# Left and right products of a two-layer pair block: token pairs side by side in the projection's columns, tokens in natural order

## The chip, the cores and the metric

One core of a Trainium2 chip runs one program. The metric is the device time of one execution in microseconds (us). The kernel before was run three times: 113.83, 113.94 and 114.15 us, median 113.94 us.

## What is computed

The input x has shape (1, 128, 128, 32), read as 128 x 128 tokens of 32 channels. Two layers follow each other; everything is float32.

```
# layer 0
x   = layernorm(x0) * ln1_w + ln1_b
left  = sigmoid(x @ left1) * (x @ left2)
right = sigmoid(x @ right1) * (x @ right2)
p   = einsum('nsre,nkre->nske', left, right)     # contraction over r, for each feature e
p   = layernorm(p) * ln2_w + ln2_b
q   = (p @ out_w) * sigmoid(x @ gate)
x1  = x0 + q
# layer 1
left = x1 @ W_left + b_left + x1 @ W_eq + b_eq
right_sum = sum over r of (x1 @ W_right + b_right)
out = left * right_sum * sigmoid(x1 @ W_gate + b_gate)
y   = layernorm(out @ W_out + b_out + x1) * ln_scale + ln_bias
```

## The kernel before

**Tiling.** The partition is r (128 rows), so `x_tok[r, s, c]` holds token s of row r in 32 neighbouring floats. The 128 tokens s are worked through in 8 chunks of 16 (`SPC`). Four tokens times 32 channels fill the 128 columns of one TensorE transpose, so a chunk is four blocks of four tokens.

**Who does what is written out by hand.** Each engine has its own program (`@block.sync`, `gpsimd`, `scalar`, `vector`, `tensor`), in which the instructions stand in the order written, and counting semaphores tie them together. No scheduler or planner moves anything. SP (the sync engine) issues the loads of x in order of the table `SUMS1` (two halves of chunk 0, then whole chunks), ACT one of them and the weights.

**First stretch, layer 0 up to the products.** For each chunk: VectorE (DVE) takes statistics of two tokens at a time (L581, `statistics1`); ACT takes square roots (L410), DVE reciprocals (L588); GpSimd (POOL) subtracts the mean (L281, `centre`) and scales (L288, `normalise1`), for the first half chunk DVE does (L608, L613); TensorE (PE) transposes the four blocks into a PSUM bank (L802, `transpose_xn`); ACT writes `xnT` to SBUF with weight and bias (L421, `affine1`); PE projects it for left and right (L817, `project_lr`), half a chunk (8 tokens) at a time; ACT takes the sigmoid of half of the columns (L431, `sigmoid_lr`); DVE multiplies the other half with it and writes `lr` (L596, `multiply_lr`). So there are 16 projections, 16 sigmoids and 16 products of 128 x 512 elements, numbered j = 2c + h for chunk c and half h. Three pairs of PSUM banks are used in turn: projection j waits until product j - 3 is done (`lr_ready`).

**One projection.** A projection has four matmuls. Each takes 64 rows of `xnT` (two tokens of 32 channels) as weights and streams `lr_blk`, 64 x 256, in which each of the two tokens has its own 128 columns: left1, right1, left2, right2, 32 columns each. The output is token by token: 128 neighbouring columns for one token.

```
596  lr[:, :, s].rearrange("p f s -> p s f")      # L596, the product's output
816  dst = bank[:, 2 + 2 * (j % 3) + t].rearrange("p (g n f) -> p n g f", g=2, n=2)[:, n]   # L817's output
```

**The layout of `lr`.** `lr[r, feature, s]` has 64 features (32 left, 32 right) and, for each, 128 neighbouring tokens, because the contraction over r (L871) takes `lr[:, e, :]` as a 128 x 128 operand: 32 matmuls of layer 0, one per feature. They wait for all 16 products (`lr_ready`, 16). The product of half a chunk thus writes 8 tokens x 64 features, feature innermost, and from one element to the next the address moves by 128 floats.

**Order of the tokens before.** So that the four matmuls of a half chunk leave their 8 tokens in order in the two banks, each chunk of 16 tokens is stored in SBUF with its 8 even tokens first and its 8 odd ones behind them (`place`, `even_first`, `stat`, `in_order`). The loads fetch even and odd tokens apart (L250, L398); everything that touches `x_tok`, `xc`, `t_tok`, the statistics of layer 0 and the columns of `xnT` lives with that order. `in_order` puts the tokens right again where the last projections write to PSUM (L967, L978, L987), in runs of 32 columns.

**After the products.** ACT copies the eight banks of p to `p_sb` (L465), DVE takes its statistics (L660), POOL (L352; chunk 0: DVE, L673) scales it and turns it to token order as `t_tok`, PE transposes it (L912) and projects it (L923), DVE adds gate and residual (L688, L697), and layer 1 follows in a loop over the 8 chunks (L992), where PE is busy most of the time. At the end the last two chunks' outputs are made by PE once more, scaled (L987), and DVE and POOL finish (L739, L785, L376).

Of the kernel before, what the change touches and what calls it, by code (L numbers as in the profile page):

```python
# [30 lines left out]
P = 128  # L31
CH = 32
GRP = P // CH
# [38 lines left out]
def place(tokens, lo, hi):  # L72

    rest = tokens.rearrange("p (m q) c -> p m q c", q=SPC // 2)
    if hi - lo < SPC:
        c, h = lo // SPC, lo % SPC // (SPC // 2)
        return rest[:, 2 * c:2 * c + 2, GRP * h:GRP * h + GRP]
    return rest[:, 2 * lo // SPC:2 * hi // SPC]


def arrived(b):

    lo, hi = SUMS1[b]
    return 32 * max(1, (hi - lo) // SPC)
# [7 lines left out]
def pair_layers(nc, x, weights, rows, out):  # L92
# [7 lines left out]
    with ExitStack() as ctx:  # L100
# [12 lines left out]
        pair_mask = sb("pair_mask", [P, 2, CH])  # L113
        lr_blk = sb("lr_blk", [P, 2, 4, CH])
# [96 lines left out]
        def halves(cols, lo, hi):  # L211

            v = cols.rearrange("p (n h k) -> p n (h k)", n=2, h=2)
            if hi - lo == SPC:
                return v
            h = lo % SPC // (SPC // 2)
            return v[:, :, h * P:(h + 1) * P]

        def even_first(features):

            return features.rearrange("p e (q n) -> p n q e", n=2)

        def stat(row, lo, hi):

            return place(row.rearrange("p (s a) -> p s a", a=1), lo, hi)

        def mean_of(lo, hi):

            v = place(stats1[:, :, 1:2], lo, hi)
            return v.to_broadcast([P, v.shape[1], v.shape[2], CH])  # L230

        def each_feature(row, lo, hi):
            v = stat(row, lo, hi)
            return v.to_broadcast([P, v.shape[1], v.shape[2], CH])
# [27 lines left out]
        def _(pool):  # L262
# [11 lines left out]
            for g in range(GRP):  # L274
                pool.wait_ge(consts, 1 + GRP + g)
                nc.gpsimd.memset(pair_mask[g * CH:(g + 1) * CH, g % 2, :], 1.0).then_inc(consts, 1)

            def centre(b):
                lo, hi = SUMS1[b]
                pool.wait_ge(stats1_ready, b + 1)  # L280
                nc.gpsimd.tensor_tensor(place(xc[:], lo, hi), place(x_tok[:], lo, hi), mean_of(lo, hi),  # L281
                                        ALU.subtract).then_inc(centred1_pool, 1)

            def normalise1(n):
# [3 lines left out]
                nc.gpsimd.tensor_tensor(place(xc[:], lo, hi), place(xc[:], lo, hi),  # L288
                                        each_feature(rstd[:, 0], lo, hi), ALU.mult).then_inc(xn_pool, 1)

            def block_diagonal(dst, src):
# [104 lines left out]
        def _(act):  # L396
            lo, hi = SUMS1[0]
            act.dma_start(place(x_tok[:], lo, hi)[:, 1], x_tok_dram[:, lo + 1:hi:2, :]).then_inc(x_in[0], 16)  # L398
# [5 lines left out]
            def root(layer, lo, hi, done):  # L404
                values, of = std[:, layer, lo:hi], st[:, layer, lo:hi]
                if layer == 0:
                    values, of = stat(std[:, 0], lo, hi), place(stats1[:, :, 2:3], lo, hi)
# [632 lines left out]
```

## Time and profile before

| | |
|---|---|
| three runs | 113.83, 113.94, 114.15 us |
| span of the profiled execution | 112.1 us |
| its own device time | not given beside the span; 1.84 us lie between the span and the median of the runs |
| PE busy | 92.5 us (83%) |
| DVE busy | 77.3 us (69%) |
| ACT busy | 66.6 us (59%) |
| POOL busy | 62.6 us (56%) |
| the 16 products (L596) on DVE | 15.9 us |
| load of x | until about 18.4 us |

The span runs from the first to the last instruction on the core. A busy share is taken over the whole span, so what a shorter instruction is worth is to be read from its own stretch: from what ends last there.

### The profile page before, as it was taken

How to read it: one execution, taken by the hardware profiler on the slowest of the kernel's cores; microseconds unless marked ns; L12 is line 12 of the kernel's file. 1: busy time of each engine (PE TensorE's matmuls, PEld its weight loads, DVE VectorE, ACT ScalarE, POOL GpSimd, SP SyncE). 2: the span in 40 equal slices, each digit the busy share in tenths (PEclk: the TensorE clock that was granted, in tenths of full speed). 3: DMA queues.
4: the chain of work that ended last, by engine and by line, in shares of the span. 5: the costliest groups of instructions: out<-in, count | busy, mean ns of one | idle time of the engine just before them, and what ended most of it. 6: DMA issues, size and time to landing. Idle time of an engine off the chain costs nothing. (4 is left out here: it accounts for less than half of the span.)

```text
span 112.1 us, 1886 instructions
## 1 busy us (share of the span) xinstructions
PE 92.5 (83%) x600; PEld 72.3 (64%) x600; DVE 77.3 (69%) x284; ACT 66.6 (59%) x110; POOL 62.6 (56%) x78
## 2 busy tenths in 40 slices
PE   1997599789999899999979999999999996495000
PEld 1994368567776799545445789878877994394000
DVE  1528697986769800599975869699979963996500
ACT  0614888687785166795499463993797399330000
POOL 5037974599950040025488585587865492699400
PEclk9999999999999999999999999999999999999955
DMA  3669997000000000000000000000023006029996
GB/s 60 126 111 171 146 146 75 0 0 0 0 0 9 0 0 0 0 0 3 0 0 0 3 6 0 0 0 6 0 35 59 0 0 94 0 34 144 147 144 100
DMA packets 33486, 4.54 MB, mean 40 GB/s; under 512 B 33348, under 2 KB 33476, under 8 KB 33476
## 3 DMA queue, kind: packets, MB, share of 16 engines
q1 hardware_dynamic: 31632, 4.00, 27.6%
q10 hardware_dynamic: 1844, 0.41, 1.8%
q8 instruction: 5, 0.08, 0.3%
q14 instruction: 5, 0.04, 0.1%
HBM read 2.31 MB, written 2.10 MB: 39 GB/s over the span
## 5 line engine op out<-in xcount | busy, mean ns | idle before, releaser
L596 DVE TENSOR_TENSOR lr<-bank,sig_lr 128x512 f32<-128x512 f32 x16 | 15.9, 1044 | 3.7 <-ACT sig_lr L431 3.7
L817 PE MATMUL bank<-lr_blk,xnT 64*128 64x256 f32 x128 | 16.5, 392 | 1.0 <-ACT xnT L421 0.7
L352 POOL TENSOR_TENSOR t_tok<-p_sb,rstd 128x512 f32<-128x512 f32 x7 | 10.2, 1462 | 11.8 <-DVE rstd L666 11.8
L360 POOL TENSOR_TENSOR x_low<-x1T,x_high 128x512 fp32r<-128x512 f32 x8 | 10.3, 1290 | 7.5 <-ACT x_high L501 7.5
L817 PEld LDWEIGHTS bank<-lr_blk,xnT 64*128 64x128 f32 x128 | 11.8, 186 | 4.0 <-issue 2.3
L660 DVE BATCH_NORM_STATS2 stats<-p_sb 128x6 f32<-128x64 f32 x64 | 8.5, 211 | 7.0 <-ACT p_sb L465 7.0
L368 POOL TENSOR_TENSOR oT<-o_a,rsum 128x512 f32<-128x512 f32 x8 | 8.7, 1089 | 6.4 <-DVE o_a L706 4.2
L431 ACT ACTIVATE sig_lr<-bank 128x512 f32<-128x512 f32 x16 | 9.6, 598 | 3.9 <-PE bank L817 3.9
L581 DVE BATCH_NORM_STATS2 stats<-x_tok 128x6 f32<-128x64 f32 x64 | 8.9, 213 | 3.5 <-DMA x_tok<-in_x 3.3
L978 PEld LDWEIGHTS bank<-wout_blk,oT 128*128 128x128 f32 x64 | 8.1, 191 | 4.0 <-POOL oT L368 3.2
L978 PE MATMUL bank<-wout_blk,oT 128*128 128x128 f32 x64 | 8.8, 281 | 2.2 <-POOL oT L368 2.2
L501 ACT ACTIVATE x_high<-x1T 128x512 fp32r<-128x512 f32 x8 | 5.0, 628 | 8.5 <-DVE x1T L697 8.4
L376 POOL TENSOR_TENSOR sq<-lr,row_rep 128x512 f32<-128x512 f32 x7 | 9.8, 1420 | 0.0
L697 DVE SCALAR_TENSOR_TENSOR x1T<-bank,w_rep,u 128x128 f32<-128x128 f32 x32 | 9.3, 347 | 0.2
L967 PE MATMUL bank<-centre_blk,x1T 128*128 128x128 f32 x64 | 8.9, 282 | 0.6 <-DVE lr L724 0.5
L288 POOL TENSOR_TENSOR xc<-xc,rstd 128x512 f32<-128x512 f32 (+1 forms) x8 | 7.9, 995 | 2.3 <-DVE rstd L588 1.9
L281 POOL TENSOR_TENSOR xc<-x_tok,stats 128x512 f32<-128x512 f32 (+1 forms) x8 | 8.1, 1012 | 1.9 <-DVE stats L581 1.8
L706 DVE SCALAR_TENSOR_TENSOR o_a<-bank,leq_bias,sig 128x512 f32<-128x512 f32 x8 | 6.0, 744 | 3.5 <-ACT sig L507 3.2
L967 PEld LDWEIGHTS bank<-centre_blk,x1T 128*128 128x128 f32 x64 | 7.8, 192 | 0.9 <-DVE lr L724 0.7
L923 PE MATMUL bank<-tT,out_blk 128*128 128x512 f32 x16 | 8.3, 598 | 0.0
L871 PE MATMUL bank<-lr 128*128 128x128 f32 x64 | 7.4, 277 | 0.5 <-DVE lr L596 0.5
L410 ACT ACT_TABLE_LOAD x6 | 7.7, 1283 | 0.1
(104 smaller groups left out, 199.8 us busy)
## 6 DMA issues: line engine op xcount, KB each, us to landing
x_tok<-in_x SPq DMA_DIRECT2D x14, 128.0 KB, 4.2
out<-sq SPq DMA_DIRECT2D x7, 256.0 KB, 3.4
x_tok<-in_x SPq DMA_DIRECT2D x3, 64.0 KB, 2.7
w_rep<-in_weights ACTq DMA_DIRECT2D x1, 180.5 KB
out<-sq ACTq DMA_DIRECT2D x1, 128.0 KB, 3.7
out<-sq SPq DMA_DIRECT2D x1, 128.0 KB, 3.8
x_tok<-in_x ACTq DMA_DIRECT2D x1, 64.0 KB, 2.7
row_rep<-in_rows ACTq DMA_DIRECT2D x1, 32.0 KB, 5.1
```

What stands on the lines that cost most here:

```text
L352: nc.gpsimd.tensor_tensor(place(t_tok[:, c % 2], 0, SPC), even_first(p_sb[:, :, s]), even_first(rstd[:, 1:2, s]).to_broadcast([P, 2, SPC / ...
L360: nc.gpsimd.tensor_tensor(x1_low[:, c % 2], x1T[:, c % 3], x1_high[:, c % 2], ALU.subtract).then_inc(x1_low_ready, 1)
L368: nc.gpsimd.tensor_tensor(oT[:, c % 2].rearrange("p (b k) -> p b k", b=BLK), o_a[:, c % 2].rearrange("p (b k) -> p b k", b=BLK), rsum[:, c ...
L376: nc.gpsimd.tensor_tensor(sq[:, s, :], yn[:, s, :], row_rep[:, 1:2, :].to_broadcast([P, SPC, CH]), ALU.add).then_inc(final, 1)
L431: nc.scalar.activation(sig_lr[:, j % 3].rearrange("p (s f) -> p s f", f=2 * CH), src[:, :, 0:2 * CH], ACT.Sigmoid).then_inc(lr_sig, 1)
L581: last = nc.vector.bn_stats(stats1[:, k:k + 2, :].rearrange("p s v -> p (s v)"), x_tok[:, k:k + 2, :].rearrange("p s c -> p c s"))
L596: nc.vector.tensor_tensor(lr[:, :, s].rearrange("p f s -> p s f"), src[:, :, 2 * CH:4 * CH], sig_lr[:, j % 3].rearrange("p (s f) -> p s f" ...
L660: last = nc.vector.bn_stats(stats2[:, k:k + 2, :].rearrange("p s v -> p (s v)"), p_sb[:, :, k:k + 2])
L697: nc.vector.scalar_tensor_tensor(out=x1T[:, c % 3, b], in0=bank[:, XT, b], scalar=vec("b_out"), in1=u[:, c % 2, b], op0=ALU.add, op1=ALU.a ...
L817: last = nc.tensor.matmul(dst, xnT[half, c, k * P:(k + 1) * P], lr_blk[half].rearrange("p g m c -> p g (m c)"), start=True, stop=True, ski ...
L967: nc.tensor.matmul(in_order(bank[:, b], j), x1T[:, c % 3, k], centre_blk[:], start=j == 0, stop=False, skip_group_check=True)
L978: last = nc.tensor.matmul(in_order(bank[:, b], j), oT[:, c % 2, k], wout_blk[:], start=False, stop=j == BLK - 1, skip_group_check=True)
```

## The change

The columns of `lr_blk` are interleaved: for each of the 128 weight columns, token 0 and token 1 of the 64 rows stand side by side (`(f g)` in place of `(g f)`). Each matmul's output is then 256 neighbouring PSUM columns, in which the two tokens of each feature are neighbours, and those two tokens are neighbours in the image too. The product writes `lr` in pairs of neighbouring tokens. Since the block order now falls out right, tokens lie in natural order everywhere, and `place`, `arrived`, `even_first` and `stat` are gone. `pair_mask` shrinks from 2 x 32 to 2 columns. The core of the diff:

```diff
-        pair_mask = sb("pair_mask", [P, 2, CH])
-        lr_blk = sb("lr_blk", [P, 2, 4, CH])
+        pair_mask = sb("pair_mask", [P, 2])
+        lr_blk = sb("lr_blk", [P, 4 * CH, 2])
...
         def in_order(bank_, j):
-            n, h = divmod(j, 2)
-            return bank_.rearrange("p (h g n c) -> p h n g c", h=2, g=GRP, n=2)[:, h, n]
+            return block_of(bank_.rearrange("p (s c) -> p s c", c=CH), j)
...
-                for first in range(lo, hi, SPC):
-                    last = min(first + SPC, hi)
-                    for n in range(2 if b else 1):
-                        sp.dma_start(place(x_tok[:], first, last)[:, n], x_tok_dram[:, first + n:last:2, :]
-                                     ).then_inc(x_in[b], 16)
+                mid = (lo + hi) // 2
+                for first, last in ((lo, mid), (mid, hi))[:2 if b else 1]:
+                    sp.dma_start(x_tok[:, first:last], x_tok_dram[:, first:last, :]).then_inc(x_in[b], 16)
...
-                nc.gpsimd.memset(pair_mask[g * CH:(g + 1) * CH, g % 2, :], 1.0).then_inc(consts, 1)
+                nc.gpsimd.memset(pair_mask[g * CH:(g + 1) * CH, g % 2:g % 2 + 1], 1.0).then_inc(consts, 1)
...
             nc.gpsimd.tensor_tensor(lr_blk[:],
-                                    w_rep[:, 0:4 * CH].rearrange("p (a m c) -> p a m c", a=1, m=4)
-                                    .to_broadcast([P, 2, 4, CH]),
-                                    pair_mask[:].rearrange("p g (a c) -> p g a c", a=1).to_broadcast([P, 2, 4, CH]),
+                                    w_rep[:, 0:4 * CH].rearrange("p (f a) -> p f a", a=1).to_broadcast([P, 4 * CH, 2]),
+                                    pair_mask[:].rearrange("p (a g) -> p a g", a=1).to_broadcast([P, 4 * CH, 2]),
                                     ALU.mult).then_inc(lr_blk_ready, 1)
...
-                nc.gpsimd.tensor_tensor(place(t_tok[:, c % 2], 0, SPC), even_first(p_sb[:, :, s]),
-                                        even_first(rstd[:, 1:2, s]).to_broadcast([P, 2, SPC // 2, CH]),
+                nc.gpsimd.tensor_tensor(t_tok[:, c % 2], p_sb[:, :, s].rearrange("p e s -> p s e"),
+                                        each_feature(rstd[:, 1], c * SPC, (c + 1) * SPC),
                                         ALU.mult).then_inc(t_ready, 1)
...
-                src = bank[:, lo:lo + 2].rearrange("p b (s f) -> p (b s) f", f=4 * CH)
-                nc.scalar.activation(sig_lr[:, j % 3].rearrange("p (s f) -> p s f", f=2 * CH),
-                                     src[:, :, 0:2 * CH], ACT.Sigmoid).then_inc(lr_sig, 1)
+                src = bank[:, lo:lo + 2].rearrange("p t (n f) -> p n t f", n=2)
+                nc.scalar.activation(sig_lr[:, j % 3].rearrange("p (n t f) -> p n t f", n=2, t=2),
+                                     src[:, :, :, 0:4 * CH], ACT.Sigmoid).then_inc(lr_sig, 1)
...
-                src = bank[:, lo:lo + 2].rearrange("p b (s f) -> p (b s) f", f=4 * CH)
+                src = bank[:, lo:lo + 2].rearrange("p t (n f g) -> p n t f g", n=2, g=2)
                 dve.wait_ge(lr_sig, j + 1)
-                nc.vector.tensor_tensor(lr[:, :, s].rearrange("p f s -> p s f"), src[:, :, 2 * CH:4 * CH],
-                                        sig_lr[:, j % 3].rearrange("p (s f) -> p s f", f=2 * CH),
+                nc.vector.tensor_tensor(lr[:, :, s].rearrange("p f (n t g) -> p n t f g", n=2, t=2), src[:, :, :, 2 * CH:4 * CH],
+                                        sig_lr[:, j % 3].rearrange("p (n t f g) -> p n t f g", t=2, n=2, g=2),
                                         ALU.mult).then_inc(lr_ready, 1)
...
-                    k = 2 * n + h
+                    k = 2 * h + n
                     for t in range(2):
                         half = slice(t * P // 2, (t + 1) * P // 2)
-                        dst = bank[:, 2 + 2 * (j % 3) + t].rearrange("p (g n f) -> p n g f", g=2, n=2)[:, n]
+                        dst = bank[:, 2 + 2 * (j % 3) + t, n * 8 * CH:(n + 1) * 8 * CH]
                         last = nc.tensor.matmul(dst, xnT[half, c, k * P:(k + 1) * P],
-                                                lr_blk[half].rearrange("p g m c -> p g (m c)"),
+                                                lr_blk[half].rearrange("p f g -> p (f g)"),
                                                 start=True, stop=True, skip_group_check=True)
```

No instruction is added, dropped or put elsewhere on any engine; only shapes change. Two places show it. On DVE, from the statistics of the last chunks (BN_STATS) to the last product and the first instruction behind it, before:

```order
L596 TENSOR_TENSOR lr<-bank,sig_lr 128x8x64
L581 BN_STATS stats<-x_tok 128x6 x24
L588 RECIPROCAL rstd<-std 128x16
L588 RECIPROCAL rstd<-std 128x32
L596 TENSOR_TENSOR lr<-bank,sig_lr 128x8x64
L588 RECIPROCAL rstd<-std 128x32
L596 TENSOR_TENSOR lr<-bank,sig_lr 128x8x64 x13
L638 TENSOR_TENSOR out_blk<-bank,mask 128x128
```

and with the change:

```order
L567 TENSOR_TENSOR lr<-bank,sig_lr 128x4x64x2
L552 BN_STATS stats<-x_tok 128x6 x24
L559 RECIPROCAL rstd<-std 128x16
L559 RECIPROCAL rstd<-std 128x32
L567 TENSOR_TENSOR lr<-bank,sig_lr 128x4x64x2
L559 RECIPROCAL rstd<-std 128x32
L567 TENSOR_TENSOR lr<-bank,sig_lr 128x4x64x2 x13
L609 TENSOR_TENSOR out_blk<-bank,mask 128x128
```

The order is the same; the product's output goes from 8 rows of 64 elements to 4 x 64 rows of 2.

On PE, the end of the projections and the start of the contraction over r (L871), before:

```order
L802 MATMUL bank<-ident,xc 128x128 x4
L817 MATMUL bank<-lr_blk,xnT 128x2x128 x16
L860 MATMUL bank<-out_scaled,centre_blk 128x32
L861 MATMUL bank<-w_rep,out_raw_blk 128x1
L863 MATMUL bank<-w_rep,leq_blk 128x1
L863 MATMUL bank<-w_rep,gate_blk 128x1
L863 MATMUL bank<-w_rep,right_blk 128x1
L871 MATMUL bank<-lr 128x128 x32
```

and with the change:

```order
L772 MATMUL bank<-ident,xc 128x128 x4
L786 MATMUL bank<-lr_blk,xnT 128x256 x16
L829 MATMUL bank<-out_scaled,centre_blk 128x32
L830 MATMUL bank<-w_rep,out_raw_blk 128x1
L832 MATMUL bank<-w_rep,leq_blk 128x1
L832 MATMUL bank<-w_rep,gate_blk 128x1
L832 MATMUL bank<-w_rep,right_blk 128x1
L840 MATMUL bank<-lr 128x128 x32
```

Here too nothing moved; a projection's matmul writes one run of 256 columns in place of two of 128.

## Rows read from the trace of the kernel before

**Rows 1.** Page, part 1 and the clock of part 2 (40 equal slices)

```profile
PE 92.5 (83%) x600; PEld 72.3 (64%) x600; DVE 77.3 (69%) x284; ACT 66.6 (59%) x110; POOL 62.6 (56%) x78
...
PEclk9999999999999999999999999999999999999955
```

**Rows 2.** Windows: busy us of each engine, PEclk, DMA share, GB/s

```profile
0.00:20.50 20.50, 15.29 (x98) 12.75 (x98) 12.70 (x75) 10.56 (x18) 11.18 (x26) 1.00 0.94 114
23.90:32.00 8.10, 8.10 (x64) 6.06 (x64) 5.68 (x6) 6.06 (x10) 7.87 (x16) 1.00 0.00 0
...
18.50:19.50 1.00, 1.00 (x12) 1.00 (x11) 1.00 (x9) 0.83 (x3) 0.40 (x1) 1.00 0.04 4
```

**Rows 3.** Timeline, DVE: start us, us, instruction, count [idle before <-what ended it]

```profile
18.38 2.14 DVE L581 BATCH_NORM_STATS2 stats<-x_tok 128x6 f32<-128x64 f32 x16 [0.63 <-DMA x_tok<-in_x]
...
24.26 1.05 DVE L596 TENSOR_TENSOR lr<-bank,sig_lr 128x512 f32<-128x512 f32 x1 [0.37 <-ACT sig_lr L431]
...
31.32 1.95 DVE L596 TENSOR_TENSOR lr<-bank,sig_lr 128x512 f32<-128x512 f32 x2 [0.55 <-ACT sig_lr L431]
33.83 2.81 DVE L596 TENSOR_TENSOR lr<-bank,sig_lr 128x512 f32<-128x512 f32 x3 [0.56 <-ACT sig_lr L431]
36.82 1.02 DVE L596 TENSOR_TENSOR lr<-bank,sig_lr 128x512 f32<-128x512 f32 x1 [0.18 <-ACT sig_lr L431]
```

**Rows 4.** Timeline, PE and its weight loads, 28 to 38 us

```profile
28.92 0.66 PE L802 MATMUL bank<-ident,xc 128*128 128x128 f32 x4
31.43 0.66 PE L802 MATMUL bank<-ident,xc 128*128 128x128 f32 x4
32.02 4.14 PE L817 MATMUL bank<-lr_blk,xnT 64*128 64x256 f32 x32
...
34.99 0.76 PEld L817 LDWEIGHTS bank<-lr_blk,xnT 64*128 64x128 f32 x8 [0.51 <-issue]
...
37.89 7.41 PE L871 MATMUL bank<-lr 128*128 128x128 f32 x64 [0.53 <-DVE lr L596]
```

**Rows 5.** Timeline, ACT, the last three sigmoids

```profile
34.06 0.60 ACT L431 ACTIVATE sig_lr<-bank 128x512 f32<-128x512 f32 x1 [0.27 <-PE bank L817]
34.93 0.60 ACT L431 ACTIVATE sig_lr<-bank 128x512 f32<-128x512 f32 x1 [0.27 <-PE bank L817]
36.19 0.60 ACT L431 ACTIVATE sig_lr<-bank 128x512 f32<-128x512 f32 x1 [0.67 <-PE bank L817]
```

**Rows 6.** Groups by form, DVE: busy us, mean ns of one | idle before

```profile
L596 DVE TENSOR_TENSOR lr<-bank,sig_lr 128x512 f32<-128x512 f32 x16 | 15.9, 1044 | 3.7 <-ACT sig_lr L431 3.7
...
L739 DVE TENSOR_TENSOR lr<-bank,rstd 128x512 f32<-128x512 f32 x1 | 0.7, 691 | 0.2 <-PE bank L987 0.2
L739 DVE TENSOR_TENSOR lr<-bank,rstd 128x256 f32<-128x256 f32 x2 | 0.8, 424 | 0.9 <-PE bank L987 0.9
L673 DVE TENSOR_TENSOR t_tok<-p_sb,rstd 128x512 f32<-128x512 f32 x1 | 1.0, 1043 | 0.0
```

**Rows 7.** Groups, DVE: the statistics of x (L581) and of p (L660)

```profile
L581 DVE BATCH_NORM_STATS2 stats<-x_tok 128x6 f32<-128x64 f32 x64 | 8.9, 213 | 3.5 <-DMA x_tok<-in_x 3.3
L660 DVE BATCH_NORM_STATS2 stats<-p_sb 128x6 f32<-128x64 f32 x64 | 8.5, 211 | 7.0 <-ACT p_sb L465 7.0
```

**Rows 8.** Timeline, POOL: the block of weights, and chunk 3's scaling

```profile
7.29 0.73 POOL L299 TENSOR_TENSOR lr_blk<-w_rep,pair_mask 128x256 f32<-128x256 f32 x1 [4.20 <-DMA w_rep<-in_weights]
...
20.76 1.05 POOL L288 TENSOR_TENSOR xc<-xc,rstd 128x512 f32<-128x512 f32 x1 [1.86 <-DVE rstd L588]
```

**Rows 9.** Groups, POOL: with and without a hop at every element

```profile
L352 POOL TENSOR_TENSOR t_tok<-p_sb,rstd 128x512 f32<-128x512 f32 x7 | 10.2, 1462 | 11.8 <-DVE rstd L666 11.8
L281 POOL TENSOR_TENSOR xc<-x_tok,stats 128x512 f32<-128x512 f32 x7 | 7.5, 1067 | 1.8 <-DVE stats L581 1.8
```

**Rows 10.** Transfers of x_tok: us from issue to landing

```profile
DMA to landing us min/median/max: 2.3/4.2/5.7
```

**Rows 11.** Timeline, PE weight loads: output in runs of 32 columns

```profile
77.33 0.97 PEld L967 LDWEIGHTS bank<-centre_blk,x1T 128*128 128x128 f32 x8
```

More of the change, by code:

```diff
@@ L69, with block_of @@
 BIAS_AT = {6: [0], 8: [1], 9: [2, 3]}
[L72 to L84, printed above, removed]
+def block_of(tokens, j):
+    return tokens[:, j * GRP:(j + 1) * GRP].rearrange("p s c -> p (s c)")
 def holding(ranges, s):
@@ L211, in halves @@
         def halves(cols, lo, hi):
[L213 to L225, printed above, removed]
+            first = lo % SPC * CH
+            return cols[:, first:first + (hi - lo) * CH]
         def mean_of(lo, hi):
-            v = place(stats1[:, :, 1:2], lo, hi)
-            return v.to_broadcast([P, v.shape[1], v.shape[2], CH])
+            return stats1[:, lo:hi, 1:2].to_broadcast([P, hi - lo, CH])
         def each_feature(row, lo, hi):
-            v = stat(row, lo, hi)
-            return v.to_broadcast([P, v.shape[1], v.shape[2], CH])
+            return row[:, lo:hi].rearrange("p (s a) -> p s a", a=1).to_broadcast([P, hi - lo, CH])
         def in_order(bank_, j):
-            n, h = divmod(j, 2)
-            return bank_.rearrange("p (h g n c) -> p h n g c", h=2, g=GRP, n=2)[:, h, n]
+            return block_of(bank_.rearrange("p (s c) -> p s c", c=CH), j)
         block = ctx.enter_context(nc.Block())
@@ L280, in centre @@
                 pool.wait_ge(stats1_ready, b + 1)
-                nc.gpsimd.tensor_tensor(place(xc[:], lo, hi), place(x_tok[:], lo, hi), mean_of(lo, hi),
+                nc.gpsimd.tensor_tensor(xc[:, lo:hi], x_tok[:, lo:hi], mean_of(lo, hi),
                                         ALU.subtract).then_inc(centred1_pool, 1)
@@ L287, in normalise1 @@
                 pool.wait_ge(centred1_pool, holding(SUMS1, lo) + 1 - OWN_CENTRE)
-                nc.gpsimd.tensor_tensor(place(xc[:], lo, hi), place(xc[:], lo, hi),
+                nc.gpsimd.tensor_tensor(xc[:, lo:hi], xc[:, lo:hi],
                                         each_feature(rstd[:, 0], lo, hi), ALU.mult).then_inc(xn_pool, 1)
@@ L397, in _ @@
             lo, hi = SUMS1[0]
-            act.dma_start(place(x_tok[:], lo, hi)[:, 1], x_tok_dram[:, lo + 1:hi:2, :]).then_inc(x_in[0], 16)
+            mid = (lo + hi) // 2
+            act.dma_start(x_tok[:, mid:hi], x_tok_dram[:, mid:hi, :]).then_inc(x_in[0], 16)
             act.dma_start(w_rep[:], weights.rearrange("(a p) n -> a p n", a=1).to_broadcast([GRP, CH, n_w])
@@ L406, in root @@
                 if layer == 0:
-                    values, of = stat(std[:, 0], lo, hi), place(stats1[:, :, 2:3], lo, hi)
+                    of = stats1[:, lo:hi, 2]
                 elif layer == 1:
@@ L575, in statistics1 @@
                 lo, hi = SUMS1[b]
-                dve.wait_ge(x_in[b], arrived(b))
-                c, half = lo // SPC * SPC, hi - lo < SPC
-                first = lo % SPC // (SPC // 2) * GRP
-                places = [c + 8 * n + first + k for n in range(2) for k in (0, 2)] if half else range(lo, hi, 2)
-                for k in places:
+                dve.wait_ge(x_in[b], 32)
+                for k in range(lo, hi, 2):
                     last = nc.vector.bn_stats(stats1[:, k:k + 2, :].rearrange("p s v -> p (s v)"),
@@ L607, in _ @@
             dve.wait_ge(stats1_ready, 1)
-            nc.vector.tensor_tensor(place(xc[:], lo, hi), place(x_tok[:], lo, hi), mean_of(lo, hi), ALU.subtract
+            nc.vector.tensor_tensor(xc[:, lo:hi], x_tok[:, lo:hi], mean_of(lo, hi), ALU.subtract
                                     ).then_inc(centre0, 1)
@@ L612, in _ @@
             dve.wait_ge(rstd1, 1)
-            nc.vector.tensor_tensor(place(xc[:], lo, hi), place(xc[:], lo, hi),
+            nc.vector.tensor_tensor(xc[:, lo:hi], xc[:, lo:hi],
                                     each_feature(rstd[:, 0], lo, hi), ALU.mult).then_inc(xn_ready, 1)
@@ L672, in _ @@
             dve.wait_ge(rstd2, 1)
-            nc.vector.tensor_tensor(place(t_tok[:, 0], 0, SPC), even_first(p_sb[:, :, 0:SPC]),
-                                    even_first(rstd[:, 1:2, 0:SPC]).to_broadcast([P, 2, SPC // 2, CH]),
+            nc.vector.tensor_tensor(t_tok[:, 0], p_sb[:, :, 0:SPC].rearrange("p e s -> p s e"),
+                                    each_feature(rstd[:, 1], 0, SPC),
                                     ALU.mult).then_inc(t0_ready, 1)
@@ L798, in transpose_xn @@
                     pe.wait_ge(xnT_ready, n - 1)
-                c = lo // SPC
-                for j in range(BLK) if hi - lo == SPC else range(lo % SPC // (SPC // 2), BLK, 2):
-                    s = c * SPC + j * GRP
-                    last = nc.tensor.transpose(bank[:, n % 2, j * P:(j + 1) * P],
-                                               xc[:, s:s + GRP, :].rearrange("p s c -> p (s c)"), ident[:])
+                c = lo // SPC * SPC
+                for j in range(lo % SPC // GRP, lo % SPC // GRP + (hi - lo) // GRP):
+                    last = nc.tensor.transpose(bank[:, n % 2, j * P:(j + 1) * P], block_of(xc[:, c:c + SPC], j), ident[:])
                 last.then_inc(xnT_ps, 1)
@@ L912, in transpose_t @@
                     last = nc.tensor.transpose(bank[:, TT, j * P:(j + 1) * P],
[L913 to L914 removed]
+                                               block_of(t_tok[:, c % 2], j), ident[:])
                 last.then_inc(tT_ps, 1)
```

9 lines of the change are left out of this document (3 added, 6 removed).

## The prediction

> **What bounds the kernel now.** I read the page's shares and slices first, then windows around the stretch that the change touches, then the timelines of DVE, PE and ACT in it, and last the groups by form for prices. The page [rows 1] shows PE 83% busy, DVE 69%, and TensorE's clock granted in full until the last two slices, so no term below comes from the clock. The 16 products, the instruction that the change is about, cost DVE 15.9 us [rows 6]. That is no gain by itself: the question is in which of three stretches DVE ends last.
>
> *Up to 20.4 us the load bounds.* The DMA share is 0.94 over 0 to 20.5 us and 0.04 from 18.5 us on [rows 2]; DVE sat idle 0.63 us for a transfer until 18.38 us, then did the statistics of the last two chunks without a break, 2.14 us [rows 3], and only then, in its own order, the reciprocals on which POOL had waited 1.86 us [rows 8]. Two products stand ahead of these statistics. Made shorter, they lengthen the wait for the transfer and nothing else.
>
> *From 23.9 to 32 us PE bounds.* PE is busy 8.10 of 8.10 us [rows 2]. The transposes of two successive chunks start 2.51 us apart (28.92, 31.43) [rows 4]. DVE's two products of a chunk take 1.95 us, and it is idle 0.56 us before the next until ACT's sigmoid, which itself comes from PE [rows 3]. So here too a shorter product only idles longer.
>
> *From 32 to 37.9 us DVE comes in at two points.* The last four projections follow one another without transposes. Projection 15 reuses the banks of product 12 and waits for it: product 12 starts at 33.83 us and takes 1.04 us [rows 3, 6], so ends at 34.87, and PE's weight loads for projection 15 start at 34.99 after 0.51 us of idle [rows 4]. The trace calls that idle "issue", but the program's only wait at this place is for product 12, and the times fit. ACT shows what it cost: it waited 0.27 us for projection 14 and 0.67 us for projection 15 [rows 5], a stall of 0.40 us. The second point is the last product itself: it starts at 36.82, right behind the last sigmoid (36.19 + 0.60), ends at 37.84, and the contraction over r starts at 37.89 [rows 3 to 5]. All 32 matmuls of it need all 16 products, so this is a full barrier, and what lies behind it moves as a block.
>
> **The change, part by part.**
>
> *The product.* Before, every element written lands 512 bytes from the one before. Its nearest neighbours are 128x512 products of the same engine: out of PSUM with everything in a row it takes 691 ns, and with 512-byte hops on the input side 1043 ns, like our 1044 [rows 6]. So one hop per element costs about 0.35 us in 512 elements, 0.69 ns a hop, on whichever side it stands. Without hops an element takes (691 - 424) / 256 = 1.04 ns. Now there are 256 hops, each behind a second element that lies next to the first. If a hop's 0.69 ns can pass beside the second element's 1.04 ns, the product takes 0.69 us; if hops add up, half of 0.35 is saved and it takes 0.87 us; if only short rows cost, it stays at 1.04 or gets longer. The bounds from rows are therefore 0.69 and 1.04 us, with a price above that as a rival. I take 0.69, because the hop is shorter than the element that could cover it.
>
> The Trainium skill bears on this choice (Vector Engine (DVE) Microarchitecture Reference, 5.2 Measured stream behaviour on trn2): a port streams at full rate when its elements come in runs of at least two adjacent 4-byte words that start on an 8-byte boundary, and any hop between such runs is free; it lists 1.71 ns per column for an output that hops at every element and 1.054 for runs of two. By that page the saving would be 0.66 ns x 512 = 0.34 us, and the sum the same within 0.02 us. The only pair-wise access that I find in the trace speaks neither way: the statistics of p read pairs of neighbouring tokens at 512-byte hops in 211 ns, the first ones read single floats 128 bytes apart in 213 ns [rows 7]; there the pairs bring nothing, or that instruction is bound by something else.
>
> *What it is worth.* Product 12 ends 0.35 us earlier, at 34.52; projection 15 starts 0.12 behind it, at 34.64 in place of 34.99. That is within the 0.40 us stall, so the whole 0.35 counts. The last sigmoid and the start of the last product move by the same 0.35; DVE is free by then (product 14 starts behind its sigmoid at 35.53 and ends at 36.22). The last product takes 0.69 in place of 1.02: another 0.33. PE's five small matmuls ahead of the barrier follow projection 15 and move with it by 0.35, ending before the product does. The small DVE instructions behind the product are unchanged. Sum: 0.35 + 0.33 = 0.68 us earlier at the barrier, 37.21 in place of 37.89. With 0.87 us it would be 2 x 0.17 = 0.34.
>
> *The other 14 products* save about 0.35 us each on DVE, some 5 us of busy time, and are worth nothing: cover is the load before 20.4 us and PE after 23.9.
>
> *The projections.* Their output is one run of 256 columns in place of two of 128. PE's four last ones run at about 0.87 us each (34.93 - 34.06, two sigmoids' starts [rows 5]; the chain of 32 instructions takes 4.14 us with the stall [rows 4]), about 0.11 us for 256 columns. I cost the change at nothing. The same for the last projections, which wrote runs of 32 columns: 8 weight loads take 0.97 us with those runs, 0.12 each [rows 11], and the contraction's 64 matmuls, which write one run each, take 7.41 us, 0.12 each [rows 4].
>
> *The weights' block.* POOL builds `lr_blk` with inner rows of 2. It takes 0.73 us now [rows 8]. POOL's own worst row against its plain one is 1462 to 1067 ns [rows 9], which would make 1.00 us of it; the lower end is today's. POOL's next work then starts up to 0.27 us late, and is covered by the idle of 1.86 us that POOL has before 20.76 us [rows 8]. Without that cover it would cost 0.27.
>
> *The loads.* The same number of transfers of the same size in the same order, from 8 neighbouring tokens in place of every second one. Floats are fetched 32 at a time either way. Cost nothing; from below and above, see the rivals. *Sigmoids, transposes, `t_tok`, centring*: the same elements with the same inner steps or fewer rows; nothing.
>
> **Against which time.** The sum is made on the profiled execution: span 112.1 - 0.7 = 111.4 us. The median of the three runs lies 1.84 us above that span; I leave that unchanged: 113.94 - 0.68 = 113.26, say 113.25 us.
>
> **The rivals.**
>
> *Hops add up* (0.87 us a product). For it: nothing in the trace shows a hop being hidden. Against: the comparison of 0.69 and 1.04 ns. Gives 113.94 - 0.34 = 113.6 us. Chance 0.12, half of it below the bound of 0.34 us.
>
> *Pairs bring nothing*, or the change does not do what it says because other hops decide. For it: the two statistics rows [rows 7]. Gives 113.9 us. Chance 0.06.
>
> *Short rows cost: DVE becomes the bound.* The product's output now has 256 rows of 2 where it had 8 of 64. If each new row costs, the price by POOL's ratio [rows 9] is 1.04 x 1.37 = 1.43 us. The point from which it decides is half of PE's 2.51 us per chunk, 1.25 us a product. Above it the 11 products from 24.26 us on [rows 3] run back to back: 11 x 1.38 (starts overlap by 0.05) = 15.2, so they end at 39.4 in place of 37.84, 1.6 us late, and the two products ahead of the last statistics add 0.8 less the idle of 0.63, 0.2 us. Gives 113.94 + 1.8 = 115.7 us: slower. Against: reading in rows of 2 costs the statistics nothing [rows 7]. Chance 0.04.
>
> *The loads land otherwise.* Before 18.4 us a transfer's landing moves everything behind it one to one when late. The median from issue to landing is 4.2 us, the slowest 5.7 [rows 10]; if the last ones land 1.5 us later, 113.25 + 1.5 = 114.75 us. Chance 0.05. Earlier landing can be used only as far as DVE is free, its idle of 0.63 us plus two shorter products, 0.7: at best 113.25 - 1.3 = 112.0 us. Chance 0.05. For either I have no row; the bytes and the number of pieces are the same.
>
> **How the numbers follow.** The forecast, 0.69 us a product and nothing else, has 0.68. A measurement of this kernel can tell about 0.3%, 0.34 us, from no change. Faster by more: 0.68 + half of the 0.12 + 0.05 for the loads, about 0.80. Within 0.3%: the other half, the 0.06 and a little of the late loads, 0.13. Slower: short rows and most of the late loads, 0.07. The three runs before spread by 0.3 us, so the forecast alone spans 113.0 to 113.5. The range for 8 in 10 has the "hops add up" and "nothing" cases inside at the upper end and a part of the early loads at the lower: 112.75 to 113.9 us.
>
> **What would show it.** In the profile after: the products' group at about 690 ns mean and 11 us busy; DVE's idle before them, 3.7 us now, grown to 8 or so; the last statistics still starting near 18.4 us, behind a longer DMA wait; the transposes still 2.51 us apart; the last sigmoid near 35.8 and the contraction over r starting near 37.2. The prediction is wrong in its price if the mean is 0.87 or more, in its covers if the mean is 0.69 but the contraction starts much earlier or later than 37.2, and in the loads if the last statistics start away from 18.4.

## The result and the profile after

Four runs of the changed kernel gave 110.46, 110.55, 110.57 and 110.65 us, median 110.56; the kernel before, run four times, has 114.05 us here. The ratio is 0.9717, with a 95% interval of 0.9694 to 0.9739. By the ratio the changed kernel is 3.2 us faster (2.8%), by the difference of the two medians 3.5; I had forecast 0.7 and had set the lower end of the range at 112.75. The span of the profiled execution went from 112.1 to 108.7 us.

I read the page of the changed kernel first: clock, DMA share and GB/s of the 40 slices, the product's group, and the two kinds of transfers.

```profile
PEclk9999999999999999999999999999999999958995
DMA  3589990000000000000000000000014006009995
GB/s 58 105 150 182 184 173 9 0 0 0 0 0 9 0 0 0 0 0 3 0 0 6 3 0 0 0 0 6 0 26 70 0 0 97 0 6 155 189 174 64
...
L567 DVE TENSOR_TENSOR lr<-bank,sig_lr 128x512 f32<-128x512 f32 x16 | 10.9, 683 | 7.2 <-ACT sig_lr L405 7.2
...
x_tok<-in_x SPq DMA_DIRECT2D x14, 128.0 KB, 3.0
out<-sq SPq DMA_DIRECT2D x7, 256.0 KB, 3.2
```

The product takes 683 ns in place of 1044, as forecast, and DVE's idle before it grew from 3.7 to 7.2 us (forecast: to 8 or so). What I had not forecast stands in the GB/s line. The kernel before had this one:

```profile
GB/s 60 126 111 171 146 146 75 0 0 0 0 0 9 0 0 0 0 0 3 0 0 0 3 6 0 0 0 6 0 35 59 0 0 94 0 34 144 147 144 100
```

Its load ran at 146 GB/s in the two full slices from 11.2 us on, and its output at 144 to 147; now the load runs at 173 to 184 and the output at 155 to 189. The bytes and the number of pieces are the same. The timeline of the changed kernel (DVE, POOL, PE; start us, us) shows what the load did:

```profile
15.43 3.16 DVE L552 BATCH_NORM_STATS2 stats<-x_tok 128x6 f32<-128x64 f32 x24
...
19.13 1.05 POOL L262 TENSOR_TENSOR xc<-xc,rstd 128x512 f32<-128x512 f32 x1 [1.44 <-DVE rstd L559]
...
33.01 0.76 PEld L786 LDWEIGHTS bank<-lr_blk,xnT 64*128 64x128 f32 x8 [0.16 <-issue]
...
34.84 0.69 DVE L567 TENSOR_TENSOR lr<-bank,sig_lr 128x512 f32<-128x512 f32 x1 [0.22 <-ACT sig_lr L405]
...
35.59 7.41 PE L840 MATMUL bank<-lr 128*128 128x128 f32 x64 [0.21 <-DVE lr L567]
```

The last three chunks' statistics follow one another without a wait for a transfer (before: 0.63 us of it until 18.38 [rows 3]), so POOL gets its reciprocals at 19.13 in place of 20.76 us [rows 8]: 1.63 us. What ends last there is now ACT. It takes the last square roots, which the reciprocals need, only at 18.45 us, behind its sigmoids and a table load:

```profile
10.95 0.32 ACT L384 ACTIVATE std<-stats,eps 128x16 f32<-128x16 f32 x1 [0.16 <-DVE stats L552]
...
18.45 0.77 ACT L384 ACTIVATE std<-stats,eps 128x16 f32<-128x16 f32 x3
```

The projections after that are as they were. The last projection starts its weight loads after 0.16 us of idle in place of 0.51 [rows 4], and the last product takes 0.69 us. The contraction over r starts at 35.59 in place of 37.89 us [rows 4], 2.30 us earlier: 1.63 from the front and 0.67 between 20 and 38 us. The latter is the forecast's 0.68.

From the contraction's start to the end of the span, 74.2 us became 73.1: another 1.1 us, in a part of the program in which the change has nothing to do but runs of columns. Windows of the last stretch, before and then changed (us, busy of each engine, PEclk, DMA share, GB/s):

```profile
102.00:104.00 2.00, 0.50 (x5) 0.31 (x3) 1.39 (x4) 0.00 (x0) 2.00 (x3) 1.00 0.97 147
104.00:106.00 2.00, 0.00 (x0) 0.00 (x0) 1.21 (x1) 0.00 (x0) 0.93 (x1) 1.00 0.96 146
106.00:108.00 2.00, 0.00 (x0) 0.00 (x0) 0.00 (x0) 0.00 (x0) 0.00 (x0) 0.69 0.97 147
```

```profile
100.00:102.00 2.00, 1.72 (x16) 1.53 (x14) 1.02 (x3) 0.00 (x0) 2.00 (x2) 1.00 1.33 204
102.00:104.00 2.00, 0.00 (x0) 0.00 (x0) 1.31 (x4) 0.00 (x0) 0.43 (x1) 1.00 1.58 177
104.00:106.00 2.00, 0.00 (x0) 0.00 (x0) 0.00 (x0) 0.00 (x0) 0.00 (x0) 0.89 1.60 172
```

(The DMA share adds up the times of packets, which can overlap, so it can pass 1.) After 106 us no compute engine works in either kernel. The output transfers are what ends last, and the span includes them. In these windows they run at 146 to 147 GB/s before and at 172 to 204 after. The output's token order did not change at all. So the token order of the loads, which the diff shows, can't be the whole cause, and something common to load and output is wanted. The order and sizes of the tiles give one: `pair_mask` went from 256 bytes per partition to 8, tiles start at multiples of 32 bytes, and every SBUF tile behind it moved down by 224 bytes. Start of the two tiles in bytes per partition (the trace holds no addresses; these come from adding up the allocations):

```
tile      before            changed
x_tok     28256 = 96 mod 128    28032 = 0 mod 128
sq        61024 = 96 mod 128    60800 = 0 mod 128
```

A transfer of x or of the output consists of pieces of 128 bytes (one token of one row).

### The profile page after: what moved, and what is told of

It is laid out like the page before. It is cut to its first block and busy times, and to the rows that moved or that the text cites. A ratio compares the mean times of both kernels' runs of the same rounds, so it can differ in the third digit from the quotient of the medians.

```text
span 108.7 us, 1886 instructions
## 1 busy us (share of the span) xinstructions
PE 92.8 (85%) x600; PEld 73.3 (67%) x600; DVE 71.3 (66%) x284; ACT 66.4 (61%) x110; POOL 62.1 (57%) x78
## 5 line engine op out<-in xcount | busy, mean ns | idle before, releaser
L786 PE MATMUL bank<-lr_blk,xnT 64*128 64x256 f32 x128 | 16.0, 390 | 1.1 <-ACT xnT L395 1.1
L567 DVE TENSOR_TENSOR lr<-bank,sig_lr 128x512 f32<-128x512 f32 x16 | 10.9, 683 | 7.2 <-ACT sig_lr L405 7.2
L945 PE MATMUL bank<-wout_blk,oT 128*128 128x128 f32 x64 | 9.7, 300 | 2.2 <-POOL oT L341 2.2
L945 PEld LDWEIGHTS bank<-wout_blk,oT 128*128 128x128 f32 x64 | 8.9, 208 | 4.0 <-POOL oT L341 3.2
L934 PE MATMUL bank<-centre_blk,x1T 128*128 128x128 f32 x64 | 8.9, 282 | 0.6 <-DVE lr L695 0.5
L934 PEld LDWEIGHTS bank<-centre_blk,x1T 128*128 128x128 f32 x64 | 7.8, 192 | 0.9 <-DVE lr L695 0.7
```

Of the source, the lines that this page charges most:

```text
L567: nc.vector.tensor_tensor(lr[:, :, s].rearrange("p f (n t g) -> p n t f g", n=2, t=2), src[:, :, :, 2 * CH:4 * CH], sig_lr[:, j % 3].rearr ...
L786: last = nc.tensor.matmul(dst, xnT[half, c, k * P:(k + 1) * P], lr_blk[half].rearrange("p f g -> p (f g)"), start=True, stop=True, skip_gr ...
L934: nc.tensor.matmul(in_order(bank[:, b], j), x1T[:, c % 3, k], centre_blk[:], start=j == 0, stop=False, skip_group_check=True)
L945: last = nc.tensor.matmul(in_order(bank[:, b], j), oT[:, c % 2, k], wout_blk[:], start=False, stop=j == BLK - 1, skip_group_check=True)
```

## The experiments

The two theories are *address* (the pieces now start at multiples of 128 bytes in SBUF) and *token order* (8 neighbouring tokens load faster than every second one). Times are medians; the kernel before had 113.8 to 114.0 us beside them.

**Old addresses.**

```diff
         pair_mask = sb("pair_mask", [P, 2])
+        pad = sb("pad", [P, 56])
```

> The changed kernel with 224 unused bytes per partition behind pair_mask, so that every later SBUF tile has the address it had before the change (x_tok and sq at 96 modulo 128 in place of 0). Address theory: the change's shrunken pair_mask moved x_tok and sq onto a 128-byte boundary, and that made the transfers faster; here the load ends near 18.4 us again, the output runs at about 146 GB/s, only the product's gain of 0.68 is left, 113.3 us. Token-order theory (8 neighbouring tokens load faster than every second one): the load keeps its 180 GB/s and the time stays near 110.6 us, 111.7 if the output alone hangs on the address.

Measured 113.11 us, ratio 0.9938 (0.9916 to 0.9959). The product is as fast as in the changed kernel, the rates are the old ones. GB/s, and the product's group:

```profile
GB/s 62 89 139 172 148 146 83 0 0 0 0 0 0 9 0 0 0 0 3 0 0 0 3 6 0 0 0 6 0 39 55 0 0 94 0 35 145 147 144 101
...
L568 DVE TENSOR_TENSOR lr<-bank,sig_lr 128x512 f32<-128x512 f32 x16 | 10.9, 684 | 7.1 <-ACT sig_lr L406 7.1
```

This is the whole change but for its addresses, and it is the kernel that my prediction had costed: 0.7 us by the ratio (0.5 to 1.0 by its interval), 0.68 forecast. In its profiled execution the contraction starts at 37.49 us, only 0.40 earlier than before, because the last statistics waited a second time for a transfer; this is taken up below.

**The kernel before, aligned.**

```diff
         pair_mask = sb("pair_mask", [P, 2, CH])
+        pad = sb("pad", [P, 8])
```

> The kernel before with 32 unused bytes per partition behind pair_mask: x_tok and sq at 0 modulo 128; tokens still even first, product still feature by feature at 1.04 us. Address theory: the load ends near 16.8 us as in the changed kernel and the output runs at 170 GB/s or more. The statistics of the last chunks no longer wait for a transfer, so the two slow products ahead of them now count with 0.35 us each, and the two at the end with 0.68 as before: changed kernel plus 1.4, 112.0 us. Token-order theory: the load ends at 18.4 us as before, 113.9 us, or 112.8 if the output gains.

Measured 111.82 us, ratio 0.9829 (0.9811 to 0.9847). 32 unused bytes in the kernel before bring 2 us, with its even and odd tokens and its slow products. Timeline of DVE and PE:

```profile
16.38 3.14 DVE L582 BATCH_NORM_STATS2 stats<-x_tok 128x6 f32<-128x64 f32 x24
...
36.90 7.41 PE L872 MATMUL bank<-lr 128*128 128x128 f32 x64 [0.54 <-DVE lr L597]
```

The statistics no longer wait for a transfer, and yet start later than in the changed kernel (16.38 against 15.43), mostly because the two slow products stand ahead of them. The contraction starts at 36.90: 0.99 us earlier than before, 1.31 later than in the changed kernel. By the medians, too, this kernel and the changed one are 1.3 us apart, twice what the products are worth without the aligned load. Not all of it is the products', though. ACT's square root that the changed kernel takes at 10.95 us stands here at 11.33, before the first product has run on DVE:

```profile
11.33 0.32 ACT L411 ACTIVATE std<-stats,eps 128x16 f32<-128x16 f32 x1 [0.15 <-DVE stats L582]
...
19.55 0.34 ACT L411 ACTIVATE std<-stats,eps 128x32 f32<-128x32 f32 x1 [0.18 <-DVE stats L582]
```

So 0.38 of the 1.31 us was there already; this point comes anywhere from 10.6 to 11.3 us in the profiles with an aligned x_tok. The other 0.93 is the 0.68 at the barrier and 0.25 from the two products ahead of the statistics: here ACT's last square root waits for them, and in the changed kernel it does not, since ACT is itself busy until then.

**Both tiles at 64 modulo 128** (the first edit with `[P, 16]`).

> The changed kernel with 64 unused bytes behind pair_mask: x_tok and sq at 64 modulo 128. If 64 bytes are the unit that counts, transfers stay fast: 110.6 us. If a piece of 128 bytes must not cross a 128- or 256-byte boundary in SBUF, the load and output are as slow as at 96 modulo 128: 113.3 us, like the first of these runs.

Measured 113.05 us, ratio 0.9933 (0.991 to 0.9957); its load runs at 145 to 147 GB/s and its output at 145. 64 bytes are not the unit: 64 and 96 modulo 128 are equally slow.

**x_tok and sq apart.** First x_tok at 96 and sq at 0:

```diff
         pair_mask = sb("pair_mask", [P, 2])
+        pad = sb("pad", [P, 56])
...
+        pad_sq = sb("pad_sq", [P, 8])
         sq = sb("sq", [P, P, CH])
```

> The changed kernel with 224 unused bytes behind pair_mask and 32 more ahead of sq: x_tok at 96 modulo 128, sq at 0. Address theory, each transfer by its own SBUF tile: the load ends as late as with the old addresses and the contraction over r starts near 37.5 us, while the output keeps its 170 GB/s or more; the changed kernel plus 1.9, 112.4 us. If something else among the moved tiles were the cause, the split would not follow x_tok and sq.

Then x_tok at 0 and sq at 96, with `pad_sq` of `[P, 24]` alone:

> The changed kernel with 96 unused bytes ahead of sq: x_tok at 0 modulo 128, sq at 96. Address theory: the load is as in the changed kernel (contraction from 35.6 us), the output runs at 146 GB/s and the end comes 1.1 us later: 111.6 us.

Measured 112.06 us (ratio 0.9852, 0.9826 to 0.9879) and 111.38 us (0.9794, 0.9772 to 0.9816). GB/s of the one and of the other:

```profile
GB/s 60 113 149 165 148 146 70 0 0 0 0 0 0 9 0 0 0 0 3 0 0 0 3 6 0 0 0 6 0 2 93 0 0 95 0 6 145 191 174 64
```

```profile
GB/s 55 119 152 175 190 158 6 0 0 0 0 0 3 6 0 0 0 0 3 0 0 3 6 0 0 0 0 6 0 68 28 0 0 96 0 47 145 147 144 100
```

Each transfer follows the address of its own tile: slow load and fast output, then fast load and slow output. Against the changed kernel x_tok's address is worth 1.5 us and sq's 0.8; together 2.3, and both off cost 2.5. I had expected 1.9 and 1.1, from the first run's profile; the direction and the place are as expected, the sizes by the medians are about a quarter smaller. The profiles say why. From the contraction's start to the end of the span it is 74.1 to 74.2 us in each of the five with sq off a multiple of 128 (this one: 109.5 - 35.35) and 73.0 to 73.1 in each of those with sq on one and the old order on POOL: sq's address is worth 1.1 us, as expected. All the rest of the scatter lies ahead of the contraction, in when the loads land, by some tenths (below), and my 1.9 was read from one execution.

**Token order in the loads alone.** SBUF in natural order, but each transfer fetches every second token, as before the change:

```diff
-                for first, last in ((lo, mid), (mid, hi))[:2 if b else 1]:
-                    sp.dma_start(x_tok[:, first:last], x_tok_dram[:, first:last, :]).then_inc(x_in[b], 16)
+                for first in range(lo, lo + 2)[:2 if b else 1]:
+                    sp.dma_start(x_tok[:, first:hi:2], x_tok_dram[:, first:hi:2, :]).then_inc(x_in[b], 16)
...
-            act.dma_start(x_tok[:, mid:hi], x_tok_dram[:, mid:hi, :]).then_inc(x_in[0], 16)
+            act.dma_start(x_tok[:, lo + 1:hi:2], x_tok_dram[:, lo + 1:hi:2, :]).then_inc(x_in[0], 16)
```

> The changed kernel (natural order in SBUF, aligned) with its loads fetching every second token, as before the change: token order in the transfers alone. Address theory: the load may end some tenths of a us later, but the statistics do not wait for it, 110.6 us. Token-order theory: the load ends near 18.4 us, 112.3 us.

The same with the 224 unused bytes of the first run:

> The changed kernel with the old addresses (x_tok and sq at 96 modulo 128) and with loads of every second token: what the change would have been without either effect on the loads. With the first of these runs (old addresses, natural order) the last statistics waited twice for a transfer, and the contraction over r started at 37.5 us, where I had forecast 37.2. If the order of the tokens caused this second wait, it is gone here: 37.2 us and 112.9 us. If it is chance in the landing of the last transfer, 37.5 us and 113.1 us.

Measured 110.50 us aligned (ratio 0.9715, against 0.9717 in natural order) and 113.29 us with the old addresses (0.9952, 0.9935 to 0.9968, against 0.9938). The token-order theory falls: the order of the loads changes neither. The last question stays a draw. In the run with old addresses and every second token, the timeline of DVE and PE reads

```profile
17.82 1.12 DVE L550 BATCH_NORM_STATS2 stats<-x_tok 128x6 f32<-128x64 f32 x8 [0.64 <-DMA x_tok<-in_x]
19.40 1.12 DVE L550 BATCH_NORM_STATS2 stats<-x_tok 128x6 f32<-128x64 f32 x8 [0.45 <-DMA x_tok<-in_x]
...
37.21 7.41 PE L838 MATMUL bank<-lr 128*128 128x128 f32 x64 [0.21 <-DVE lr L565]
```

The contraction starts where I had forecast it for the change, at 37.21, but the second wait is there too, so the order is not its cause: the four profiles of the changed kernel with x_tok at 64 or 96 modulo 128 start the contraction at 36.91, 37.21, 37.47 and 37.49 us, in each 16.7 us after the last statistics end, and these end by when the last transfers land. In the kernel before, the statistics end at 20.52 us as they do in this run (18.38 + 2.14 [rows 3]; 19.40 + 1.12), and the contraction starts at 37.89. With the landing equal, the products are worth 0.68 us, the sum that I had forecast.

**0 modulo 256** (the first edit with `[P, 32]`).

> The changed kernel with 128 unused bytes behind pair_mask: x_tok and sq at 0 modulo 256 in place of 128 modulo 256. A piece of a transfer has 128 bytes; with either address none crosses a 128- or a 256-byte boundary, so by the address theory nothing changes: 110.6 us, load and output as in the changed kernel. If the place within 256 bytes counts beside that, one of the two rates moves.

Measured 110.75 us, ratio 0.9722 (0.9689 to 0.9755): the same as at 128 modulo 256.

**Pairs on odd words.** What makes the product's pairs cheap is a separate question:

```diff
-        lr = sb("lr", [P, 2 * CH, P])
+        lr_room = sb("lr_room", [P, 2 * CH * P + 8])
+        lr = lr_room[:, 1:1 + 2 * CH * P].rearrange("p (f s) -> p f s", s=P)
...
```

The tiles `y` and `yn`, which lie over `lr` later, keep their places.

> The changed kernel with lr moved by one float (4 bytes), so that each pair that the product writes begins on an odd word and straddles an 8-byte boundary; y and yn stay where they were. If a pair is cheap because it fills one aligned 8-byte word, the product loses part or all of its gain: 0.8 to 1.04 us in place of 0.68, and the time rises by 2 to 4 products' worth, 0.5 to 1.4 us. If the pair is cheap only because its two elements follow each other, the product stays at 0.68 us and the time at 110.6.

The product's group in this run:

```profile
L569 DVE TENSOR_TENSOR lr_room<-bank,sig_lr 128x512 f32<-128x512 f32 x16 | 13.6, 853 | 5.2 <-ACT sig_lr L407 5.2
```

And the contraction in its timeline:

```profile
36.03 1.16 PE L842 MATMUL bank<-lr_room 128*128 128x128 f32 x8 [0.36 <-DVE lr_room L569]
```

One run, 110.97 us; the group has the product at 853 ns, between 683 and 1044, and the contraction starts 0.44 us later than in the changed kernel. Pairs that each fill one aligned 8-byte word are cheap; pairs on odd words lose half of the gain on average. Whether each loses half is not shown: of these pairs every second one also crosses a multiple of 16 bytes, and if only those lost all of it the mean would be (683 + 1044) / 2 = 864 ns, close to 853 as well.

**What the aligned transfers uncover.** Two edits on the changed kernel, first on DVE's order:

```diff
-            multiply_lr(0, 0)
             statistics1(5)
-            multiply_lr(0, 1)
+            multiply_lr(0, 0)
             statistics1(6)
+            multiply_lr(0, 1)
```

> The changed kernel with DVE's order changed at two places: the statistics of the fifth and sixth whole chunk (indices 5 and 6) each go ahead of the product that stood before them. With the aligned load DVE no longer waits for the last transfers; it idles 0.68 us for the first sigmoid with statistics queued behind the product. If DVE now sets the end of this stretch, that idle is filled and the contraction over r starts 0.4 to 0.7 us earlier: 110.0 us. If the transfers still set it, the wait comes back as a wait for x_tok and the time stays at 110.6.

Measured 110.22 us, ratio 0.9682 (0.9652 to 0.9712, which overlaps the changed kernel's 0.9694 to 0.9739), and the contraction from 35.27 us in place of 35.59. The idle of 0.68 us is gone, and a wait of 0.26 us for x_tok has come in its place. But the 0.32 us are not the edit's. ACT's timeline in this run:

```profile
10.63 0.32 ACT L384 ACTIVATE std<-stats,eps 128x16 f32<-128x16 f32 x1 [0.21 <-DVE stats L552]
...
18.13 0.77 ACT L384 ACTIVATE std<-stats,eps 128x16 f32<-128x16 f32 x3
```

ACT's square root for the statistics ahead of the edited place comes at 10.63 in place of 10.95 us, so the 0.32 us were gained before it; from there to the last square roots it is 7.50 us, and to the contraction 24.64 us, both as in the changed kernel. DVE's order buys nothing, because ACT ends last in this stretch. My two cases, DVE or the transfers, had left ACT out.

Then POOL's order:

```diff
-BIAS_AT = {6: [0], 8: [1], 9: [2, 3]}
+BIAS_AT = {6: [0], 8: [1], 9: [3]}
...
+                if i == CHUNKS + 1:
+                    bias3(2)
                 if i >= 3 and i % 2:
                     times_right(i - 2)
```

> The changed kernel with POOL's last addition for chunk 2 moved ahead of the last multiplication with right_sum, into the 3.0 us for which POOL waits there (its input is ready since 87.1 us). Its output transfer then leaves at about 92.3 us in place of 97.1. If the end is set by the output transfers, which now have one chunk of 256 KB less in the last 10 us, the kernel ends about 1.5 us earlier: 109.1 us. If the end is set by the chain of PE and DVE up to the last half chunk (issued at 103.3 us), it stays at 110.6.

Measured 109.25 us, ratio 0.9595 (0.9551 to 0.9638), as expected (109.1). The contraction starts at 35.76 us, no earlier than in the changed kernel, and the rest of the span takes 71.5 us in place of 73.1. Timeline of POOL:

```profile
91.05 1.28 POOL L349 TENSOR_TENSOR sq<-lr,row_rep 128x512 f32<-128x512 f32 x1
94.12 1.42 POOL L341 TENSOR_TENSOR oT<-o_a,rsum 128x512 f32<-128x512 f32 x1 [1.80 <-DVE o_a L679]
```

The page's GB/s in its 40 slices:

```profile
GB/s 56 109 140 182 189 187 11 0 0 0 0 0 9 0 0 0 0 0 3 0 0 0 3 6 0 0 0 6 0 0 98 0 0 23 118 55 88 174 175 61
```

The addition for chunk 2 lies in POOL's gap (3.02 us of idle, now 1.80), its 256 KB leave at 92 us, and the burst at the end is a chunk shorter. That the end comes earlier although no compute engine works faster shows that the output transfers set it.

> Both of the last two edits together. If each works on its own end, the gains add: 110.6 - 0.5 - 1.5 = 108.6 us. If moving the front by 0.5 us only presses the output together again, it is 109.1 us.

Both edits together: 109.18 us, ratio 0.958 (0.953 to 0.9629), the same as the second alone. Its profile has the contraction from 35.86 us, again 24.6 us behind ACT's square root (11.23), and 71.5 us from there to the end, as with the second edit alone. So nothing was lost in the output: the first edit had no gain to add, at neither end. The second edit alone is the version to take: it beats both kernels, by 4.7 and by 1.3 us.

## Why the prediction was wrong, point by point

- **The product, 0.69 us with pairs: right.** 683 ns. The argument from rows (a hop of 0.69 ns passes beside an element of 1.04 ns) picked the right end. The rule of the Trainium skill (Vector Engine (DVE) Microarchitecture Reference, 5.2 Measured stream behaviour on trn2) agrees: its figures for an output that hops gave a saving of 0.34 us, measured 0.36. Its condition on the 8-byte boundary, of which I had made nothing, counts here too: 853 ns without it, in one run.
- **Its worth at the barrier, 0.35 + 0.33: right for the kernel that I costed.** The stall ahead of the last projection and the last product gave 0.67 us in the changed kernel's trace and 0.68 at the old addresses with the landing equal, and the change at its old addresses is 0.6% faster (0.7 us by the ratio).
- **"Cost nothing" for the loads: the step that failed.** I looked at what the transfers fetch (bytes, pieces, tokens) and not at where they put it. The diff's line on `pair_mask`, which I cited as a smaller mask, moved x_tok and sq by 224 bytes. The term that I put at nothing measured 1.5 us by x_tok's address alone. The sign that I had named for it came: the last statistics start well ahead of 18.4 us.
- **The output was not in the working at all.** The last windows of the trace before had a DMA share of 0.97 with idle engines, and I had read that stretch only for the clock. sq's address measured 0.8 us by the medians and 1.1 by the profiles. A change at the end of the program seemed impossible, since nothing there was edited but the runs of columns.
- **The cover over the two early products held only with the slow load.** I had said that shortening the products ahead of the last statistics lengthens the wait for the transfer and nothing else. With the aligned load that wait is gone: before-but-aligned to changed is 1.31 us at the contraction in place of 0.68. Of that surplus 0.25 us is these two products' and 0.38 was there before them, in those two executions. The rival on early landing had this term (idle of 0.63 and 0.7 of products, at best 112.0 us) but at a chance of 0.05 and with nothing for the output; it was the nearest to what happened and still 1.4 us short.
- **Projections, block of weights, clock: right.** Transposes stay 2.51 us apart (24.78, 27.29, 29.80 in the changed kernel), the weights' block took 0.61 us, less than its 0.73, and matmuls in runs of 32 or 128 columns cost the same (a mean of 282 ns for L967 before and for its counterpart L934 now).

By the ratios the parts sum up like this: product alone 0.7 us, addresses alone 2.0 us (0.9829), and 0.5 us more when both come together; in sum 3.2. Of the 0.5 the profiles show 0.25 as the two products that the faster load uncovers; the rest is not told apart from the scatter in when the loads land.

## What to carry to other kernels

A diff changes the addresses of every tile behind an allocation that it resizes: before costing it, list the SBUF addresses of the tiles that transfers write or read, modulo the size of their pieces, for both kernels. Where pieces are as small as 128 bytes, put such tiles at multiples of 128; an unused column or two costs nothing and brought 2 us of 114 here. And a cost that is "covered by the load" is covered only as long as the load is slow: price it a second time without that cover, and ask which other engine ends last then. Here it was ACT, and a reordering of DVE's work bought nothing.

## What the runs showed of the hardware

- **Pieces of 128 bytes and their place in SBUF.** In the 40 slices of the profiles, once a load or an output is well under way and until it ends, the load of x and the output of sq run at 144 to 148 GB/s when the tile starts at 64 or 96 modulo 128 (the load of one run, with every second token, at 155 and 139) and at 169 to 192 when it starts at 0, in both directions, each by its own tile. Multiples of 128 and of 256 are equal. Early on the difference is not there: the load of the kernel before reached 183 GB/s at 9 to 10 us, and the first full slice of the output has 144 to 158 GB/s whatever the address, as long as POOL's order is the old one. So the address shows only after some us of load or output, and no run here tells why. Windows of the kernel before:

```profile
9.00:10.00 1.00, 1.00 (x9) 0.67 (x9) 0.65 (x6) 0.31 (x1) 0.70 (x2) 1.00 1.22 183
...
12.00:13.00 1.00, 0.79 (x6) 0.42 (x4) 0.95 (x7) 1.00 (x1) 1.00 (x1) 1.00 1.59 145
```

The Trainium skill (DMA: Bandwidth & Descriptors, How a descriptor splits into AXI transactions) says, by the vendor's account, that a transaction holds at most 256 bytes and must start at a multiple of 256, and that the bytes between that start and the piece's own are fetched unused and still cost beats. By that rule half of the pieces at 64 or 96 would cross such a border and need two transactions, which agrees in sign; its beats would give 8 and 9 per piece for 64 and 96 against 6 at 0, an estimate from that page, but here 64 and 96 are alike and the ratio is about 1.25 (182 to 146 GB/s). At 64 or 96 every piece crosses a multiple of 128 and every second one a multiple of 256, at 0 none crosses either, so which border decides, no run here tells.
- **Writes in pairs.** One element per 512-byte hop 1044 ns, an aligned pair per hop 683 (as fast as everything in a row, 691 [rows 6]), pairs on odd words 853 (one run).
- **The clock fell in the tail of the changed kernel and it cost nothing.** PE's eight matmuls at 95.44 us ran with the granted clock at its lower level, 1.2 GHz, where before it was 2.4 GHz. Their timeline row in the changed kernel:

```profile
95.44 2.07 PE L945 MATMUL bank<-wout_blk,oT 128*128 128x128 f32 x8 [1.59 <-POOL oT L341]
```

And the window around them, with the granted clock of 0.50 behind the engines' busy times:

```profile
95.40:97.50 2.10, 2.06 (x9) 2.06 (x10) 2.10 (x3) 0.00 (x0) 2.10 (x2) 0.50 0.04 8
```

In the kernel before, and in the run with pairs on odd words, the same eight took 1.16 us after the same idle of 1.59 us. From the contraction's start to the end of the span it is 73.1 us in the changed kernel (108.7 - 35.59) and 73.1 in the run with pairs on odd words (109.1 - 36.03): the eight matmuls' 0.91 us did not reach the end, which the output transfers set.
